# Self-attention's causal mask written into PSUM by TensorE instead of added by VectorE

## The chip, the cores and the metric

The kernel runs on one core of one Trainium2 chip. The metric is the device time of one execution in microseconds; the time given for a kernel is the median of several executions.

## What is computed

Three layers are applied to x (8 sequences of 64 tokens, width 512): a decoder block, a delta-rule attention layer and a mixture of experts. The change touches only the first part of the decoder block, its causal self-attention with 16 heads of width 32:

```
q, k, v = x @ Wq, x @ Wk, x @ Wv + bv          # per head
scores = (q @ k.T) * 32 ** -0.5
scores = where(tril(ones(64, 64)), scores, -inf)
p = softmax(scores)
sa = p @ v
x = layernorm(sa + x, g1, be1)
```

After it come cross-attention to 1601 tokens of context, a feed-forward layer, the delta-rule layer and the experts. All data are float32.

## The kernel before, in words

Every engine runs a list of instructions written out by hand, and semaphores join the lists; nothing is reordered by a planner. Of this kernel only the functions `pe_self`, `dve_self` and `act_self` matter here. They hold the list of TensorE (PE), of VectorE (DVE) and of ScalarE (ACT) for self-attention.

The 512 tokens are taken in four tiles, t = 0 to 3, of 128 tokens: a tile is two sequences, `j` = 0 and 1. The 16 heads are split as 4 blocks of width 128 (`c`) of 4 heads (`i`). The scores of a tile stand in `sc`, which is four PSUM banks: bank `i` holds, in its first 256 columns, the heads `(i, c)` side by side, 64 columns each, and the rows 0 to 63 are the first sequence, 64 to 127 the second. So one tile's scores are 128 rows by 1024 values.

For one tile the steps are:

1. `scores(t)` on PE: 32 small matmuls write the 16 heads of two sequences into `sc` (L368). There is one set of banks, so PE may start the next tile only after VectorE has read this one: it waits for `s1_masked`.
2. `shifted(t)` on DVE, three instructions: scores plus mask, from PSUM into `s1` in SBUF (L258); the negated maximum of each row and head (L261, `nmax`); `s1` plus that maximum (L262), which releases `s1_ready`.
3. `exponentials(t)` on ACT: `p1` = exp of `s1` (L312).
4. `turn_probs(t)` on PE: eight transposes of `p1` into the two ring banks (L384); ACT copies them to `pT1` (L327).
5. `outputs(t)` on PE: small matmuls with the values (L399) into the banks `turnbank` and `pv`.
6. `normalised(t)` on DVE: reciprocal and product (L276, L277), the residual (L282), layernorm statistics (L163, L164), and the affine part (L177, L181), with two small GpSimd (POOL) steps for the root in between (L168, L169). It releases `normed`.

PE's list is: projections of q and k (L358), `scores(0)`, `values(0)`, `values(1)` (the projection of v, L374), `scores(1)`, `values(2)`, `values(3)`, and then for t = 0 to 3 `turn_probs(t)`, `scores(t + 2)` while there is one, `outputs(t)`. Behind it stand two early pieces of cross-attention's key projection (L598) and the transposes of the normed tiles (L423), which wait for `normed`.

DVE's list is: `shifted(0)`, a split of a weight matrix, copies of the values, `shifted(1)`, copies of the values, and then for t = 0 to 3 `shifted(t + 2)` while there is one, `normalised(t)`. ACT's list has, in its loop over t, the copies to `pT1` first and `exponentials(t + 2)` behind them.

The mask is built early by GpSimd in SBUF: 0 where a token may look and -3.0e38 elsewhere, 128 rows by 4 x 64 columns, so it is right for one bank as it stands. `ident` is a 128 by 128 identity in SBUF, used by every transpose.

Of the kernel before, what the change touches and what calls it, by code (L numbers as in the profile page):

```python
# [16 lines left out]
ALU = mybir.AluOpType  # L17
ACT = mybir.ActivationFunctionType
AX = mybir.AxisListType

P = 128
B, S, D = 8, 64, 512
TOK = B * S
NT = TOK // P
NC = D // P
H, E = 16, 32
# [4 lines left out]
G = 256  # L31
# [11 lines left out]
def build(nc, a, out):  # L43
# [4 lines left out]
    def sem(name):  # L48
        if name not in sems:
            sems[name] = ctx.enter_context(nc.semaphore(name))  # L50
        return sems[name]
# [3 lines left out]
    def at(name, offset, shape, dt=F32):  # L55
        return nc.alloc_sbuf_tensor_at(name, shape, dt, offset=base + offset)


    sc = ctx.enter_context(nc.psum_tensor("sc", [P, 4, 512], F32))
# [6 lines left out]
    ident = at("ident", 0, [P, P])  # L66
# [38 lines left out]
    kT1 = at("kT1", R + 8192, [P, NC, TOK])  # L105
# [3 lines left out]
    mask = at("mask", R + 79872, [P, NC, S])  # L109
# [9 lines left out]
    s1 = at("s1", R + 188992, [P, 1024])  # L119
# [27 lines left out]
    def over_tiles(v, n=NT):  # L147

        return v.unsqueeze(1).to_broadcast([v.shape[0], n, v.shape[1]])

    def over_width(v, w):

        return v.unsqueeze(2).to_broadcast([v.shape[0], v.shape[1], w])
# [8 lines left out]
    def norm_stats(dve, link, src, t):  # L162
        link(dve.bn_stats(stat[:, t, :], src[:, t, :]))  # L163
        dve.bn_aggr(mv[:, t, :], stat[:, t, :]).then_inc(sem("variance_ready"), 1)  # L164
# [6 lines left out]
    def norm_apply(dve, n, dst, src, t):  # L171

        dve.wait_ge(sem("rstd_ready"), norm_count(n, t))
        return dve.tensor_scalar(dst[:, t, :], src[:, t, :], mv[:, t, 0:1], rstd[:, t:t + 1], ALU.subtract, ALU.mult)
# [8 lines left out]
    def norm_affine(dve, link, n, dst, src, t, gain, shift):  # L183

        dve.wait_ge(sem("variance_ready"), norm_count(n, t))
        link(norm_center(dve, src, t, gain))
        return norm_shift(dve, n, dst, src, t, shift)
# [32 lines left out]
    def values_copies(eng, copy, t):  # L220

        eng.wait_ge(sem("self_proj_done"), 2 * NC + t + 1)
        for dst, to, of in ((v1, 0, 0), (v1s, 0, S), (v1s, S, 0)):
            n = P if dst is v1 else S
            copy(dst[to:to + n, t, :, 0:E], bank[4 + t][of:of + n, :].rearrange("p (h e) -> p h e", h=H))\
                .then_inc(sem("v1_copied"), 1)

    def dve_self(dve, link):
        dve.wait_ge(sem("x_loaded"), 16)
        for t in range(NT):  # L230
            norm_stats(dve, link, xin, t)
        for t in range(NT):
            norm_apply(dve, 0, xa, xin, t).then_inc(sem("normed"), 1)

        for c in (0, 1):
            dve.wait_ge(sem("turned"), 1)
            dve.tensor_copy(nT[:, c, :], bank[c]).then_inc(sem("turned_copied"), 1)
        dve.wait_ge(sem("rows_loaded"), 64)
        dve.wait_ge(sem("normed"), NT)
        link(dve.tensor_tensor(xa[:, :, :], xa[:, :, :], over_tiles(bv1[:, :]), ALU.add))  # L240
        for c in (0, 1):
            dve.wait_ge(sem("self_proj_done"), c + 1)
            dve.tensor_scalar(qT1[:, c, :], bank[c], SCALE, None, ALU.mult).then_inc(sem("self_qk_copied"), 1)
        dve.wait_ge(sem("split_high"), 1)
        dve.tensor_tensor(wk_l[:, :, :], wk2[:, :, :], wk_h[:, :, :].bitcast(F32), ALU.subtract).then_inc(sem("split_low"), 1)
        for c in (0, 1):
            dve.wait_ge(sem("self_proj_done"), NC + c + 1)
            dve.tensor_copy(kT1[:, c, :], bank[4 + c]).then_inc(sem("self_qk_copied"), 1)

        nmax16 = nmax[:, :, :].rearrange("p a b -> p (a b)")  # L250

        def shifted(t):
            dve.wait_ge(sem("scores_done"), t + 1)
            if t > 0:
                dve.wait_ge(sem("p1_ready"), t)
            else:
                dve.wait_ge(sem("mask_ready"), 2)
            dve.tensor_tensor(s1[:, :].rearrange("p (i k) -> p i k", i=4), sc[:, :, 0:G],  # L258
                              over_tiles(mask[:, :, :].rearrange("p c k -> p (c k)"), 4), ALU.add).then_inc(sem("s1_masked"), 1)
            dve.wait_ge(sem("s1_masked"), t + 1)  # L260
            link(dve.tensor_reduce(nmax16, s1[:, :].rearrange("p (h k) -> p h k", h=H), AX.X, ALU.max, negate=True))  # L261
            dve.tensor_tensor(s1[:, :].rearrange("p (h k) -> p h k", h=H), s1[:, :].rearrange("p (h k) -> p h k", h=H),  # L262
                              over_width(nmax16, S), ALU.add).then_inc(sem("s1_ready"), 1)

        shifted(0)
        dve.wait_ge(sem("split_high"), 2)
        dve.tensor_tensor(wv_l[:, :, :], wv2[:, :, :], wv_h[:, :, :].bitcast(F32), ALU.subtract).then_inc(sem("split_low"), 1)
        values_copies(dve, dve.tensor_copy, 0)
        shifted(1)
        values_copies(dve, dve.tensor_copy, 2)  # L270

        def normalised(t):
            dve.wait_ge(sem("outputs_done"), 2 * (t + 1))
            for q in (0, 1):
                out = bank[6 + q][:, 0:8 * (E + 1)].rearrange("p (m e) -> p m e", e=E + 1)
                link(dve.reciprocal(rinv[:, q, :], out[:, :, E]))  # L276
                dve.tensor_tensor(sa[:, t, :].rearrange("p (m q n) -> p m q n", m=2, q=2)[:, :, q, :].rearrange("p m (i e) -> p m i e", i=4),  # L277
                                  out[:, :, 0:E].rearrange("p (m i) e -> p m i e", m=2),
                                  rinv[:, q, :].rearrange("p (m i) -> p m i", m=2).unsqueeze(3).to_broadcast([P, 2, 4, E]),
                                  ALU.mult).then_inc(sem("sa_written"), 1)  # L280
            dve.wait_ge(sem("sa_written"), 2 * (t + 1))
            link(dve.tensor_tensor(sa[:, t, :], sa[:, t, :], xa[:, t, :], ALU.add))  # L282
            norm_stats(dve, link, sa, t)
            norm_affine(dve, link, 1, xa, sa, t, g1[:, :], be1[:, :]).then_inc(sem("normed"), 1)

        for t in range(NT):
            if t + 2 < NT:
                shifted(t + 2)
            normalised(t)
        dve_jobs(dve, EARLY)  # L290
        for c in (0, 1):
            dve.wait_ge(sem("turned"), 2)
            dve.tensor_copy(nT[:, c, :], bank[c]).then_inc(sem("turned_copied"), 1)
# [51 lines left out]
    def pe_self(pe):  # L345
# [14 lines left out]

        def scores(t):
            if t > 0:
                pe.wait_ge(sem("s1_masked"), t)
            for c in range(NC):
                for j in (0, 1):
                    for i in range(4):
                        rows, b = slice(E * i, E * i + E), 2 * t + j
                        m = pe.matmul(sc[S * j:S * j + S, i, c * S:(c + 1) * S], qT1[rows, c, b * S:(b + 1) * S],  # L368
                                      kT1[rows, c, b * S:(b + 1) * S], start=True, stop=True)
            m.then_inc(sem("scores_done"), 1)  # L370

        def values(t):
# [30 lines left out]

        pe.wait_ge(sem("self_qk_copied"), 2 * NC)
        scores(0)
        pe.wait_ge(sem("matrix2_loaded"), 16)
        values(0)
        values(1)
        scores(1)
        values(2)  # L410
        values(3)
        for t in range(NT):
            turn_probs(t)
            if t + 2 < NT:
                scores(t + 2)
            outputs(t)
# [402 lines left out]
    def dve_jobs(dve, jobs):  # L819

        for k in jobs:
            if k % 2:
                dve.wait_ge(sem("job_done"), k + 1)
                dst, src = job_views(k)
                dve.tensor_copy(dst, src).then_inc(sem("job_copied_v"), 1)  # L825
# [1399 lines left out]
```

## Time and profile before

| | |
|---|---|
| median of 3 runs | 1516.21 us (1515.05 to 1517.49) |
| time of the profiled execution | 1516.03 us |
| its span in the trace | 1514.8 us |
| PE busy | 1455.1 us, 96% |
| DVE busy | 746.1 us, 49% |
| ACT busy | 561.8 us, 37% |
| share of TensorE in the chain that ended last | 88% |

The span runs from the first to the last instruction in the trace, and 1.2 us lie around it. A busy PE is one that has an instruction in it, not one at its peak. The "PEclk" line is TensorE's granted clock in tenths of full speed.

### The profile page before, as it was taken

The numbers are of one execution on the slowest core, as the hardware profiler recorded it, in microseconds if no ns is written. First come the engines' busy times: TensorE is split into PE (matmuls) and PEld (weight loads), VectorE is DVE, ScalarE is ACT, GpSimd is POOL, SyncE is SP. The second block draws the span as 40 slices with busy tenths as digits, with TensorE's granted clock in tenths as the row PEclk, the third lists the DMA queues.
The fourth block names the chain that finished last, engine by engine and source line by source line (L and its number), as shares of the span: only waits on it lengthen the run. The fifth ranks groups of instructions, "written<-read, shape, count | busy, mean of one in ns | idle before, by whom it ended". The sixth has DMA issues, their size and how long they took to land.

```text
span 1514.8 us, 30228 instructions
## 1 busy us (share of the span) xinstructions
PE 1455.1 (96%) x12960; PEld 1066.0 (70%) x12960; DVE 746.1 (49%) x1288; ACT 561.8 (37%) x1179; POOL 253.1 (17%) x290
## 2 busy tenths in 40 slices
PE   9799899999999999999999998998989999999998
PEld 5469788888888888888878776786478744444444
DVE  3632232443544544535346466545976544444444
ACT  1323333344343443434444444451523133333332
POOL 1223222212121212121212230602061000000000
PEclk9889999999999999999999999999999999999999
DMA  7012211010101010101011035305100069999992
GB/s 263 2 35 89 67 46 43 22 46 22 47 22 43 26 43 22 47 22 46 22 43 47 24 129 200 105 0 211 39 3 30 32 219 347 347 347 347 348 346 83
DMA packets 85218, 159.97 MB, mean 106 GB/s; under 512 B 4576, under 2 KB 25056, under 8 KB 85088
## 3 DMA queue, kind: packets, MB, share of 16 engines
q1 hardware_dynamic: 85088, 158.06, 29.9%
q8 instruction: 104, 1.70, 0.5%
q14 instruction: 26, 0.21, 0.0%
HBM read 157.00 MB, written 1.05 MB: 104 GB/s over the span
## 4 chain that ended last, share of the span: by engine, by line
PE 88%; DVE 7%; ACT 2%; POOL 2%; issue 1%; DVEq 0%; ACTq 0%; POOLq 0%
PE ring L598 18%; PE ring L608 18%; PE ring L1972 7%; PE turnbank L644 6%; PE pv L2027 6%; PE pv L1972 4%; PE sc L625 4%; PE pv L663 3%; PE sc L1572 3%; PE sc L1140 3%; PE ring L1152 1%; POOL x_l L562 1%; PE sc L2043 1%; PE sc L358 1%; PE sc L431 1%
## 5 line engine op out<-in xcount | busy, mean ns | idle before, releaser
L562 POOL TENSOR_TENSOR x_l<-raw,x_h 128x384 fp32r<-128x384 f32 (+1 forms) x160 | 162.4, 1047 | 696.6 <-ACT x_h L555 696.4
L598 PE MATMUL ring<-x_h,wk_h 128*128 128x384 f32 (+1 forms) x512 | 186.9, 365 | 5.5 <-POOL x_l L562 5.5
L608 PE MATMUL ring<-wv_h,x_h 128*128 128x512 f32 (+2 forms) x520 | 191.4, 368 | 0.0
L752 ACT ACTIVATE prob<-sc,nm 128x384 f32<-128x384 f32 (+1 forms) x256 | 154.0, 612 | 98.7 <-DVE nm L846 56.5
L608 PE MATMUL ring<-wv_h,x_l 128*128 128x512 f32 (+2 forms) x520 | 181.6, 349 | 0.0
L608 PE MATMUL ring<-wv_l,x_h 128*128 128x512 f32 (+2 forms) x520 | 181.0, 348 | 0.0
L841 DVE TENSOR_REDUCE nm<-sc 128x2 f32<-128x898 f32 (+1 forms) x128 | 128.0, 1021 | 102.4 <-PE sc L625 102.4
L598 PE MATMUL ring<-x_h,wk_l 128*128 128x384 f32 (+1 forms) x512 | 177.2, 346 | 0.0
L598 PE MATMUL ring<-x_l,wk_h 128*128 128x384 f32 (+1 forms) x512 | 176.9, 346 | 0.0
L644 PE MATMUL turnbank<-ident,prob 128*128 128x128 f32 x880 | 137.0, 278 | 12.9 <-DVE pT L832 7.1
L832 DVE COPY pT<-turnbank 128x512 f32<-128x512 f32 x126 | 86.7, 688 | 101.6 <-PE turnbank L644 101.2
L644 PEld LDWEIGHTS turnbank<-ident,prob 128*128 128x128 f32 x880 | 103.1, 141 | 28.3 <-issue 9.2
L598 PEld LDWEIGHTS ring<-x_h,wk_h 128*128 128x128 f32 x512 | 97.6, 191 | 30.9 <-issue 29.2
L608 PEld LDWEIGHTS ring<-wv_h,x_h 128*128 128x128 f32 (+1 forms) x520 | 96.4, 185 | 27.6 <-issue 16.6
L1972 PE MATMUL ring<-w_raw,disp 128*64 128x512 f32 (+1 forms) x640 | 115.0, 596 | 0.0
L608 PEld LDWEIGHTS ring<-wv_h,x_l 128*128 128x128 f32 (+1 forms) x520 | 96.3, 185 | 14.7
L608 PEld LDWEIGHTS ring<-wv_l,x_h 128*128 128x128 f32 (+1 forms) x520 | 96.7, 186 | 11.4 <-issue 0.2
L598 PEld LDWEIGHTS ring<-x_l,wk_h 128*128 128x128 f32 x512 | 97.7, 191 | 1.6
L598 PEld LDWEIGHTS ring<-x_h,wk_l 128*128 128x128 f32 x512 | 97.3, 190 | 1.8
L742 ACT COPY pT<-turnbank 128x512 f32<-128x512 f32 x94 | 55.1, 586 | 96.7 <-PE turnbank L644 96.1
L825 DVE COPY v<-ring 128x512 f32<-128x512 f32 (+3 forms) x65 | 38.0, 584 | 106.1 <-PE ring L608 106.1
L825 DVE COPY kT<-ring 128x384 f32<-128x384 f32 (+1 forms) x64 | 36.7, 574 | 99.5 <-PE ring L598 99.3
(475 smaller groups left out, 2324.6 us busy)
## 6 DMA issues: line engine op xcount, KB each, us to landing
w_raw<-in_ew SPq DMA_DIRECT2D x96, 1024.0 KB, 11.1
raw<-in_ctxT SPq DMA_DIRECT2D x30, 768.0 KB, 4.3
raw<-in_ctxT SPq DMA_DIRECT2D x10, 900.0 KB, 4.7
wf1b<-in_wf SPq DMA_DIRECT2D x1, 2560.0 KB, 10.6
wf2b<-in_wf SPq DMA_DIRECT2D x1, 2560.0 KB, 16.8
wf1a<-in_wf SPq DMA_DIRECT2D x1, 1536.0 KB, 9.4
wf2a<-in_wf SPq DMA_DIRECT2D x1, 1536.0 KB, 12.8
xin<-in_x SPq DMA_DIRECT2D x1, 1024.0 KB, 5.7
```

The lines of the kernel that those rows point to most:

```text
L562: pool.tensor_tensor(x_l[x % 3][:, c, 0:w], raw[x % 3][:, c, 0:w], x_h[x % 2][:, c, 0:w].bitcast(F32), ALU.subtract)\
L598: m = pe.matmul(ring[k % 2][:, 0:w], wt[:, c, e:e + P], xt[:, c, 0:w], start=c == 0 and n == 0, stop=c == NC - 1 and n == 2)
L608: m = pe.matmul(ring[k % 2][0:rows, 0:cols.stop - cols.start], xt[:, c, t1:t1 + rows], wt[:, c, cols], start=c == 0 and n == 0, stop=c == ...
L625: m = pe.matmul(sc[S * j:S * j + S, i, FIRST[r]:FIRST[r] + w], qT[rows, c, b * S:(b + 1) * S], kT[b % 2][rows, c, BASES[r][j]:BASES[r][j] ...
L644: m = pe.transpose(turned_bank(i)[0:w, s * P:(s + 1) * P], prob[:, head, t0:t0 + w], ident[:, :])
L742: act.copy(dst, src).then_inc(sem("turned_a"), 1)
L752: act.activation(prob[:, i, 0:WIDTHS[r]], sc[:, i, score_columns(r)], ACT.Exp, bias=nm[:, b % 2, r, h:h + 1], accum_out=psum[:, b % 2, r, ...
L825: dve.tensor_copy(dst, src).then_inc(sem("job_copied_v"), 1)
L832: dve.tensor_copy(dst, src).then_inc(sem("turned_v"), 1)
L841: ins = dve.tensor_reduce(new, sc[:, 2 * i:2 * i + 2, score_columns(r)], AX.X, ALU.max, negate=True)
L1972: k = pe.matmul(out, disp[:, c, columns], w_raw[n % NSLOT][:, c, :], start=c == 0, stop=c == NC - 1)
L2027: k = pe.matmul(down_bank[0:CAP, :], ht[:, 4 * q + f, :], wt[:, f, :], start=q == 0 and f == 0 and i == 0, stop=q == 3 and f == 3 and i == 2)
```

## The change

Before each tile's scores, TensorE now writes the mask into the four banks: one matmul for each bank, with the identity as the weights and the mask as the moving operand, 128 rows by 256 columns. The 32 small score matmuls then add to what stands in the bank (start is false). VectorE's addition of the mask is gone: the maximum is taken from PSUM, and the difference is formed from PSUM into `s1`. The banks are now free for the next tile only after that last step, so PE waits for `s1_ready` in place of `s1_masked`; the wait for `p1_ready` stands before the difference and not before the first instruction.

```diff
         def shifted(t):
             dve.wait_ge(sem("scores_done"), t + 1)
+            by_head = sc[:, :, 0:G].rearrange("p i (c k) -> p i c k", c=NC)
+            link(dve.tensor_reduce(nmax16, by_head, AX.X, ALU.max, negate=True))
             if t > 0:
                 dve.wait_ge(sem("p1_ready"), t)
-            else:
-                dve.wait_ge(sem("mask_ready"), 2)
-            dve.tensor_tensor(s1[:, :].rearrange("p (i k) -> p i k", i=4), sc[:, :, 0:G],
-                              over_tiles(mask[:, :, :].rearrange("p c k -> p (c k)"), 4), ALU.add).then_inc(sem("s1_masked"), 1)
-            dve.wait_ge(sem("s1_masked"), t + 1)
-            link(dve.tensor_reduce(nmax16, s1[:, :].rearrange("p (h k) -> p h k", h=H), AX.X, ALU.max, negate=True))
-            dve.tensor_tensor(s1[:, :].rearrange("p (h k) -> p h k", h=H), s1[:, :].rearrange("p (h k) -> p h k", h=H),
-                              over_width(nmax16, S), ALU.add).then_inc(sem("s1_ready"), 1)
+            dve.tensor_tensor(s1[:, :].rearrange("p (i c k) -> p i c k", i=4, c=NC), by_head,
+                              over_width(nmax16, S).rearrange("p (i c) k -> p i c k", i=4), ALU.add).then_inc(sem("s1_ready"), 1)
...
         def scores(t):
             if t > 0:
-                pe.wait_ge(sem("s1_masked"), t)
+                pe.wait_ge(sem("s1_ready"), t)
+            else:
+                pe.wait_ge(sem("mask_ready"), 2)
+            for i in range(4):
+                pe.matmul(sc[:, i, 0:G], ident[:, :], mask[:, :, :].rearrange("p c k -> p (c k)"), start=True, stop=False,
+                          skip_group_check=True)
             for c in range(NC):
                 for j in (0, 1):
                     for i in range(4):
                         rows, b = slice(E * i, E * i + E), 2 * t + j
                         m = pe.matmul(sc[S * j:S * j + S, i, c * S:(c + 1) * S], qT1[rows, c, b * S:(b + 1) * S],
-                                      kT1[rows, c, b * S:(b + 1) * S], start=True, stop=True)
+                                      kT1[rows, c, b * S:(b + 1) * S], start=False, stop=True, skip_group_check=True)
```

On TensorE, from the last value projections to the first outputs, the list before is this (one row for each kind of instruction, with what it waits for; `ring<-ident,p_101` are the transposes of `turn_probs(0)`, and L399 is where `outputs(0)` begins):

```order
L374 MATMUL ring<-w_in_98,nT 128x512 x7
L368 MATMUL sc<-kT_91,qT_90 64x64 [waits s1_masked]
L368 MATMUL sc<-kT_91,qT_90 64x64 x31
L374 MATMUL turnbank<-w_in_98,nT 128x512 x4
L374 MATMUL pv<-w_in_98,nT 128x512 x4
L384 MATMUL ring<-ident,p_101 128x128 [waits v1_copied,p1_ready]
L384 MATMUL ring<-ident,p_101 128x128 x7
L368 MATMUL sc<-kT_91,qT_90 64x64 [waits s1_masked]
L368 MATMUL sc<-kT_91,qT_90 64x64 x31
L399 MATMUL turnbank<-v_105,pT_108 64x33 [waits ones_ready,probs_copied]
```

In the changed kernel the same place on TensorE reads so:

```order
L375 MATMUL ring<-w_in_98,nT 128x512 x7
L363 MATMUL sc<-mask,ident 128x256 [waits s1_ready]
L363 MATMUL sc<-mask,ident 128x256 x3
L369 MATMUL sc<-kT_91,qT_90 64x64 x32
L375 MATMUL turnbank<-w_in_98,nT 128x512 x4
L375 MATMUL pv<-w_in_98,nT 128x512 x4
L385 MATMUL ring<-ident,p_101 128x128 [waits v1_copied,p1_ready]
L385 MATMUL ring<-ident,p_101 128x128 x7
L363 MATMUL sc<-mask,ident 128x256 [waits s1_ready]
L363 MATMUL sc<-mask,ident 128x256 x3
L369 MATMUL sc<-kT_91,qT_90 64x64 x32
L400 MATMUL turnbank<-v_105,pT_108 64x33 [waits ones_ready,probs_copied]
```

Four mask matmuls stand before each tile's scores, behind the same instructions as the scores before; nothing else on TensorE has moved.

On VectorE, `shifted(2)` and the beginning and the end of `normalised(0)` stand in the list before as follows:

```order
L258 TENSOR_TENSOR s_107<-sc,mask 128x1024 [waits p1_ready,scores_done]
L261 TENSOR_REDUCE nmax<-s_107 128x16 [waits s1_masked]
L262 TENSOR_TENSOR s_107<-s_107,nmax 128x1024 [waits dve_chain]
L276 RECIPROCAL rinv<-turnbank 128x8 [waits outputs_done]
...
L181 SCALAR_TENSOR_TENSOR xa<-sa,rstd,be_94 128x512 [waits rstd_ready,dve_chain]
L258 TENSOR_TENSOR s_107<-sc,mask 128x1024 [waits p1_ready,scores_done]
```

In the changed kernel the same stretch of VectorE's list is this:

```order
L255 TENSOR_REDUCE nmax<-sc 128x16 [waits scores_done]
L258 TENSOR_TENSOR s_107<-sc,nmax 128x1024 [waits p1_ready,dve_chain]
L272 RECIPROCAL rinv<-turnbank 128x8 [waits outputs_done]
...
L181 SCALAR_TENSOR_TENSOR xa<-sa,rstd,be_94 128x512 [waits rstd_ready,dve_chain]
L255 TENSOR_REDUCE nmax<-sc 128x16 [waits scores_done]
```

One instruction of three is gone from each tile, and the order of the others is as it was.

## Rows read from the trace of the kernel before

**Rows 1.** The page: busy time, the granted clock in 40 slices, the chain's shares.

```profile
PE 1455.1 (96%) x12960; PEld 1066.0 (70%) x12960; DVE 746.1 (49%) x1288; ACT 561.8 (37%) x1179; POOL 253.1 (17%) x290
...
PEclk9889999999999999999999999999999999999999
...
PE 88%; DVE 7%; ACT 2%; POOL 2%; issue 1%; DVEq 0%; ACTq 0%; POOLq 0%
```

**Rows 2.** Busy time by stretch; columns: stretch, length, engines' busy time, clock, DMA.

```profile
0.00:58.00 58.00, 54.37 (x296) 29.84 (x296) 27.01 (x33) 13.54 (x15) 6.22 (x22) 1.00 0.51 172
58.00:92.40 34.40, 23.47 (x459) 21.52 (x459) 24.61 (x44) 9.79 (x16) 12.67 (x16) 0.70 0.02 4
92.40:1514.80 1422.40, 1377.22 (x12208) 1014.69 (x12206) 694.45 (x1212) 538.44 (x1149) 234.18 (x253) 0.99 0.30 105
```

**Rows 3.** The chain that ended last, 40 to 95 us; start, length, what.

```profile
42.28 0.91 PE sc L368 x53
43.19 7.06 PE ring L374 x16
...
54.73 3.45 PE pv L374 x8
...
60.14 1.11 PE ring L384 x8
61.24 1.24 PE sc L368 x60
...
62.50 1.24 DVE s L258
...
65.02 1.50 DVE s L262
66.52 0.13 DVE rinv L276
...
71.63 1.23 DVE s L258
...
75.41 0.94 issue
76.35 1.06 ACT pT L327 x2
...
84.40 6.21 PE ring L598 x24
90.61 1.75 PE sc L423 x16
```

**Rows 4.** Timeline, DVE and POOL, 43 to 91 us; start, length, instruction.

```profile
43.23 1.23 DVE L258 TENSOR_TENSOR s<-sc,mask 128x1024 f32<-128x1024 f32 x1 [7.76 <-PE sc L368]
...
44.48 1.22 DVE L261 TENSOR_REDUCE nmax<-s 128x16 f32<-128x1024 f32 x1
...
45.74 1.23 DVE L262 TENSOR_TENSOR s<-s,nmax 128x1024 f32<-128x1024 f32 x1
...
63.48 1.96 POOL L562 TENSOR_TENSOR x_l<-raw,x_h 128x384 fp32r<-128x384 f32 x2
...
90.16 0.75 DVE L181 SCALAR_TENSOR_TENSOR xa<-sa,rstd,be 128x512 f32<-128x512 f32 x1 [0.82 <-POOL rstd L169]
```

**Rows 5.** Timeline of PE: matmuls that bound the price of the new ones.

```profile
1.58 8.81 PE L343 MATMUL pv<-ident 128*128 128x128 f32 x56 [1.58 <-POOL ident L201]
...
92.31 0.28 PE L608 MATMUL ring<-wv_l,x_h 128*128 128x256 f32 x1
92.43 0.28 PE L608 MATMUL ring<-wv_h,x_l 128*128 128x256 f32 x1
```

**Rows 6.** Busy time and granted clock (third from last) by stretch, as Rows 2.

```profile
60.14:61.03 0.89, 0.89 (x8) 0.82 (x8) 0.00 (x0) 0.89 (x1) 0.89 (x2) 1.00 0.00 0
61.03:67.85 6.82, 6.48 (x202) 5.57 (x200) 5.17 (x8) 2.73 (x5) 4.29 (x5) 0.50 0.02 5
170.26:173.67 3.41, 3.41 (x14) 3.16 (x12) 0.56 (x1) 0.00 (x0) 0.00 (x0) 0.50 0.02 5
173.67:177.09 3.42, 3.42 (x38) 2.38 (x40) 2.16 (x3) 1.46 (x4) 0.00 (x0) 1.00 0.00 0
```

## The prediction, made before the changed kernel ran

> **What bounds the kernel now.** I read the page first: TensorE is busy for 96% of the span and holds 88% of the chain that ended last, VectorE 7% [rows 1]. That average says nothing of self-attention, which lies in the first 92 us. The busy time by stretch shows three stages [rows 2]. Up to 58 us TensorE has 54.4 us of work in 58. From 58.0 to 92.4 us it has 23.5 in 34.4, at a mean clock of 0.70, and VectorE has more than it, 24.6. From 92.4 us to the end TensorE is full again (1377 of 1422 us). So a delay that reaches 92.4 us is handed on whole: behind it one dense list of TensorE runs to the end, and the context loads that it needs start from `normed`, so they move along with it. What the change is worth is what it does to the time of the last transposes (L423).
>
> The chain of work in this piece gives the path [rows 3]. From 42.28 to 58.18 us it is TensorE alone: `scores(0)` 0.91 us, values 7.06, `scores(1)` and the rest of the values, the last of them 54.73 + 3.45. ScalarE's copies of the last values lead to `turn_probs(0)` at 60.14 and `scores(2)` at 61.24. At 62.50 the path goes over to VectorE: `shifted(2)` (62.50 to 66.52), `normalised(0)` (66.52 to 71.63), `shifted(3)` (71.63 to 75.37). Then the chain goes by ScalarE and TensorE, whose copies to `pT1` are queued behind `exponentials(3)`; but VectorE works on beside it without a gap that matters, and its last `normed` comes at 90.16 + 0.75 = 90.91 [rows 4], when TensorE's early projections (84.40 + 6.21 = 90.61) are just done. Both ways begin at the end of `shifted(3)`, so they shift as one.
>
> **The change part by part.** The path to 92.4 us has four pieces that change.
>
> *Mask matmuls of tiles 0 and 1.* They stand in the stretch where TensorE alone is the path, behind a wait that ends where it ended before, and nothing covers them. What does a matmul of 256 float32 columns with the full array cost? The trace shows no such instruction. It shows a float32 matmul as two records; with 512 columns eight records take 3.45 us, 0.431 each [rows 3]. From below: the 256-column matmuls of L608, on numbers rounded for the fast pass, follow each other at 92.43 - 92.31 = 0.12 us with one record each, so four masks would cost 0.48 us [rows 5]. From above: the keep-busy matmuls, float32 with the identity as weights and 128 columns, take 8.81 / 56 = 0.157 us a record, more than a quarter of 0.431; if 128 more columns add another 0.108, a record is 0.265 and four masks cost 8 x 0.265 = 2.12 us. The nearest row is the plain float32 matmul of the same engine on the same kind of data, and half its columns are 0.215 us, which is above the 0.157 that loading the identity seems to need. I take 0.215: eight records are 1.72 us for a tile, 3.44 us for two. VectorE's saving in these tiles is on no path: `s1_ready` of tile 1 is not waited for until 60.14.
>
> *Mask matmuls of tile 2.* They stand between `turn_probs(0)` and `scores(2)`, on the path again. At full clock they are 1.72 us. But the granted clock is 1.00 (2.4 GHz) from 60.14 to 61.03 and 0.50 (1.2 GHz) from 61.03 to 67.85, after TensorE stood idle from 58.2 to 60.1 and during the transposes [rows 6]. The idle piece and the transposes are the same in the changed kernel, 3.44 us later, so the fall comes about at the end of the transposes and the masks run at half clock. Dense full-array matmuls got the clock back sooner than the small ones here: from 170.26 it was at half for 3.41 us and then full [rows 6]. So of the eight records at 0.43 us, 3.2 us go at half clock and the last half record at full; that is 3.3 us. `scores(2)` then takes 0.91 as in tile 0 and not 1.24: 0.33 back [rows 3]. The value is 3.3 - 0.33 = 3.0 us. Bounds: 1.72 - 0.33 = 1.4 if the clock stays full, and 3.43 if half clock outlasts it all.
>
> The Trainium skill's page "TensorE: Matmul & The Clock Gate" (section on PE-mode transpose) says that transposes don't count as activity for the clock gate. The trace agrees in that the clock fell 0.9 us into the transposes. By that rule the masks, which are no transposes, would be the first work that counts after the idle piece; it changes no term.
>
> *Mask matmuls of tile 3.* These I cost at nothing. `scores(3)` now waits for the end of `shifted(2)`, then needs 1.72 + 0.91 us, or 3.43 + 1.28 = 4.7 at half clock. What hides it is `normalised(0)` on VectorE, 71.63 - 66.52 = 5.11 us, which stands ahead of `shifted(3)`. Queued behind the wait is `outputs(1)`; it ends some 75 us into the span at the latest, and VectorE asks for it only after `shifted(3)`, at about 79. Without that cover the cost would be the whole 1.7 to 3.4 us.
>
> *VectorE's savings.* Two of the four `shifted` are on the path, tiles 2 and 3. Each loses one instruction of three: 63.76 - 62.50 and 72.88 - 71.63, 1.25 us from start to start, 2.5 us for the two. Is the rest slower from PSUM? The three forms take 1.23 (from PSUM), 1.22 and 1.23 us (both from SBUF) [rows 4], so I add nothing. L262 of tile 2 took 1.50 us beside a split on GpSimd that ran until 65.44 [rows 4]; by my times that split ends before, so 0.27 us more is saved: 2.8 us in all. From below the saving is 2.5.
>
> The Trainium skill's page "VectorE: DVE Perf Modes" (section on the errata) gives VectorE a fixed cost of 120 cycles with a source in PSUM and of 58 from SBUF. The mask addition from PSUM against the difference from SBUF shows 0.00 us in this trace, not 0.065. By the page the four instructions from PSUM would add 4 x 0.065, less the one that was there in each tile: an estimate of 0.13 us more.
>
> *Sum.* 3.44 + 3.0 - 2.8 = +3.6 us. Against the profiled execution's own 1516.03 us that gives 1519.6; the median of the runs is 0.2 us above that execution, which I leave aside.
>
> **The rivals.**
>
> *The clock stays up at tile 2 (not slower).* Whether the clock falls before, in or behind the masks hangs on a moment that can lie otherwise than in the one execution that I see: the three runs are 2.4 us apart. With the masks and `scores(2)` at full clock the sum is 3.44 + 1.4 - 2.8 = +2.0 us, 1518.0. It decides below +3.03 us (0.2% of 1516, about what can be told from no change): that is when less than about half of the masks fall on half clock. For it: the masks are dense, and begin 1.1 us after the idle piece ends. Against it: the clock fell exactly there before.
>
> *The masks cost more than half of a 512-column matmul.* At 0.265 us a record, as bounded above, tiles 0 and 1 cost 4.24 us and tile 2 some 0.4 more: 3.6 + 0.8 + 0.4 = +4.8, 1520.8. Against it: the identity's own load seems to need no more than 0.157 us.
>
> *The masks are nearly free.* At 0.12 us for a whole matmul, tiles 0 and 1 cost 0.96 us and tile 2 about 0.5 to 1.0, and the VectorE savings win: 0.96 + 0.7 - 2.8 = -1.1, 1514.9. Against it: every plain float32 matmul in the trace shows two records at four times the pace of the rounded ones. Even with masks at nothing the gain is no more than 2.8 to 3.1 us, so "faster by over 0.2%" needs them free and something more.
>
> *The moved wait becomes the bound.* If the masks of tile 3 run at half clock and at the higher price (4.2 + 1.28 = 5.5 us against 5.11), `shifted(3)` starts 0.4 us late: 3.6 + 1.2 + 0.4 = +5.2, 1521.2.
>
> **How the numbers follow.** The first forecast has 0.52, with +3.2 to +4.1 as its own range (3.4 for tile 2 at most, and the small doubt on the 0.27); an execution where the clock falls midway lies between it and the full-clock rival, which has 0.28. The higher price has 0.09, the nearly free masks 0.06, the late wait 0.05. The range is 1517.4 to 1521.4: it takes in the first two, the higher price, and a microsecond either way for the spread of the runs. What a measurement of this kernel can tell from no change is about 0.2%, 3.03 us. Slower by more: most of the first (0.40 of 0.52, since 3.6 lies near the limit), the higher price and the late wait, with 0.01 of the second: 0.53. Faster by more: 0.03, from the nearly free masks and what I don't see. Within 0.2%: 0.44.
>
> **What would show it.** In the changed kernel's trace: (1) the four masks of tiles 0 and 1 are eight records each, 0.215 us from start to start, and `turn_probs(0)` starts at about 63.6 us; (2) the masks of tile 2 begin at about 64.7 us with the granted clock at 0.50, `scores(2)` ends at about 68.9; (3) `shifted` is two instructions of 1.22 to 1.23 us; (4) `shifted(3)` starts straight behind `normalised(0)`, not behind a wait for TensorE; (5) the last transposes start about 3.6 us later than 90.61. The prediction is wrong if the clock behaves otherwise in (2), if reading PSUM twice costs VectorE more, or if the stage behind 92.4 us takes up the delay, for which I see no room.

## The result, and the profile after

| | before | changed |
|---|---|---|
| median, 12 runs each | 1515.93 us (1515.05 to 1517.49) | 1518.74 us (1517.76 to 1521.63) |
| profiled execution | 1516.03 us | 1518.77 us |
| its span | 1514.8 us | 1517.5 us |

The ratio is 1.002 with a 95% interval of 1.0012 to 1.0028: the change costs 2.8 us, and between 1.8 and 4.2 us by the interval. Against the limit of 0.2% it is neither clearly within nor clearly beyond it.

The chain of work of the changed kernel, from 40 to 98 us (start, length, what), answers to [rows 3]:

```profile
42.48 1.99 PE sc L363 x8
...
45.32 7.06 PE ring L375 x16
52.38 1.73 PE sc L363 x8
...
65.06 1.73 PE sc L363 x8
...
67.67 1.24 DVE nmax L255
...
68.93 1.22 DVE s L258
...
75.26 1.23 DVE nmax L255
...
76.51 1.24 DVE s L258
...
86.78 6.24 PE ring L599 x24
93.02 1.75 PE sc L424 x16
94.77 1.43 PE ring L609 x12
```

Three groups of mask matmuls (L363) are on it, and VectorE's part is two steps for each tile. The last transposes start at 93.02 instead of 90.61, 2.41 us later. Its steps in order: 0.20 us later already at 42.48, before anything is changed (the 13 traces of this document reach this place between 42.11 and 42.54); the stretch from there to the values (45.32) is 2.84 us and was 0.91, so tile 0 costs 1.93; tile 1 costs 1.73 in the same way; from `turn_probs(0)` (64.00) to VectorE's start (67.67) it is 3.67 us and was 2.36, so tile 2 costs 1.31; `shifted(2)` is 1.54 us shorter (67.67 to 70.15, before 62.50 to 66.52) and `shifted(3)` 1.25. The sum is 0.20 + 1.93 + 1.73 + 1.31 - 1.54 - 1.25 = +2.38 us, and 0.03 more at the transposes. The span is 2.7 us longer. Most of the other 0.3 us appears at one place: at 1195.8 us VectorE sits idle for 0.27 us between two of its own instructions, and for 0.03 us at the same place before. Why is open.

The groups of instructions of self-attention after the change (line, engine, operation, tiles, count, busy time, mean ns of one, idle before) show the new prices beside [rows 4] and [rows 5]:

```profile
L363 PE MATMUL sc<-mask,ident 128*128 128x256 f32 x32 | 7.8, 386 | 1.2 <-ACT kT L302 0.7 <-DVE s L258 0.5
...
L258 DVE TENSOR_TENSOR s<-sc,nmax 128x1024 f32<-128x1024 f32 x4 | 4.9, 1224 | 0.1
L255 DVE TENSOR_REDUCE nmax<-sc 128x16 f32<-128x1024 f32 x4 | 4.9, 1222 | 19.5 <-PE sc L369 19.5
```

The reduction and the difference from PSUM take 1.22 us each, as they did from SBUF. The granted clock is the third number from the end in the busy time by stretch; these two rows answer to [rows 6]:

```profile
64.00:77.12 13.12, 10.68 (x296) 8.96 (x296) 8.35 (x13) 4.34 (x6) 5.21 (x6) 1.00 0.01 2
77.12:90.77 13.65, 9.77 (x149) 9.24 (x150) 11.41 (x26) 3.09 (x5) 2.68 (x4) 0.50 0.01 3
```

In this execution the clock did not fall at tile 2. It stayed at 2.4 GHz through the masks, and fell to 1.2 GHz at 77.12, while TensorE stood idle (75.2 to 79.8). It waited there for ScalarE's copies, which are queued behind `exponentials(3)` and so behind `shifted(3)`.

### The profile page after: what moved, and what is told of

It reads as the page before. It is cut to its first block, busy times and chain, and to the rows that moved or that the text cites. A ratio compares the mean times of both kernels' runs of the same rounds, so it can differ in the third digit from the quotient of the medians.

```text
span 1517.5 us, 30288 instructions
## 1 busy us (share of the span) xinstructions
PE 1460.7 (96%) x12992; PEld 1070.2 (71%) x12992; DVE 741.3 (49%) x1284; ACT 561.8 (37%) x1179; POOL 252.2 (17%) x290
## 4 chain that ended last, share of the span: by engine, by line
PE 88%; DVE 7%; ACT 2%; POOL 2%; issue 1%; DMA 0%; DVEq 0%; ACTq 0%
PE ring L599 18%; PE ring L609 18%; PE ring L1973 7%; PE turnbank L645 6%; PE pv L2028 6%; PE pv L1973 4%; PE sc L626 4%; PE pv L664 3%; PE sc L1573 3%; PE sc L1141 3%; PE ring L1153 1%; POOL x_l L563 1%; PE sc L2044 1%; PE sc L354 1%; PE sc L432 1%
```

## The experiments

Where a run's difference is called that of the median, it is against the kernel before in the same series (1516.47 us for the first four, 1515.99 for the next four); where it is called that of the trace, it is the start of the transposes of the normed tiles against 90.61.

### TensorE's part alone

The mask matmuls are added to the kernel before, and VectorE keeps its addition.

```diff
-MASKED = -3.0e38
+MASKED = -1.0e38
...
             if t > 0:
                 pe.wait_ge(sem("s1_masked"), t)
+            else:
+                pe.wait_ge(sem("mask_ready"), 2)
+            for i in range(4):
+                pe.matmul(sc[:, i, 0:G], ident[:, :], mask[:, :, :].rearrange("p c k -> p (c k)"), start=True, stop=False,
+                          skip_group_check=True)
...
-                                      kT1[rows, c, b * S:(b + 1) * S], start=True, stop=True)
+                                      kT1[rows, c, b * S:(b + 1) * S], start=False, stop=True, skip_group_check=True)
```

> The mask matmuls are added and VectorE keeps its own addition too, so the mask is added twice (its fill is -1.0e38 here, so that the sum stays finite; the output is the same). My theory: TensorE's part alone costs 3.7 us at tiles 0 and 1 and 1.3 us (full clock) to 3.0 us (half clock) at tile 2, so +5.0 to +6.7 us against the kernel before. The rival that the cost lies in VectorE's reads of PSUM expects no more than +3 us here. A granted clock of 0.50 on the masks of tile 2 in this profile, against 1.00 in the changed kernel's, would speak for the moment of the fall lying differently from execution to execution.

Measured: 1521.63 us, +5.2 by the median, ratio 1.0032 (1.0023 to 1.0041). In its chain of work the last transposes start at 95.51, +4.9:

```profile
65.11 1.73 PE sc L367 x8
...
67.72 1.24 DVE s L258
...
70.24 1.23 DVE s L262
...
95.51 1.75 PE sc L428 x16
```

The last `normed` is +4.95: 0.26 of a later start at 42.54 (42.28 before), 1.93 + 1.73 + 1.31 from TensorE, less 0.27 from L262, which takes 1.23 us here and 1.50 before: GpSimd's split, which ran beside its first 0.42 us before, ends here at 69.36, before it starts. The cost of the change is TensorE's.

### VectorE's part alone

`shifted` as changed, and TensorE as before; no mask is applied.

```diff
         def shifted(t):
             dve.wait_ge(sem("scores_done"), t + 1)
+            by_head = sc[:, :, 0:G].rearrange("p i (c k) -> p i c k", c=NC)
+            link(dve.tensor_reduce(nmax16, by_head, AX.X, ALU.max, negate=True))
...
         def scores(t):
             if t > 0:
-                pe.wait_ge(sem("s1_masked"), t)
+                pe.wait_ge(sem("s1_ready"), t)
```

> VectorE's part alone: two instructions from PSUM, and no mask matmuls on TensorE, so the mask is left out of the computation. My theory: tiles 2 and 3 save 1.25 us each, and 0.27 us where the difference no longer stands beside GpSimd's split: -2.5 to -2.8 us. The rival that reading PSUM twice costs VectorE more than SBUF (0.13 us in all by the Trainium skill) expects -2.4 us; a rival in which VectorE is not the path in this stage expects 0.

Measured: 1511.85 us, -4.6 by the median, ratio 0.9966 (0.9953 to 0.9979). This is more than expected. The median rests on five runs; the profiled execution is 4.2 us faster than the profiled one of before, 3.96 of it at the start of the last transposes. The chain of work and the clock by stretch say where these are from:

```profile
61.91 1.24 DVE nmax L255
...
69.50 1.23 DVE nmax L255
...
81.01 5.64 PE ring L594 x24
86.65 1.75 PE sc L419 x16
```

```profile
59.97:73.52 13.55, 7.08 (x280) 6.14 (x280) 10.39 (x18) 5.85 (x9) 5.24 (x6) 1.00 0.01 2
73.52:83.76 10.24, 8.51 (x145) 7.99 (x146) 8.16 (x19) 1.59 (x4) 2.69 (x4) 0.50 0.01 4
```

VectorE starts tile 2 at 61.91, 0.59 us earlier: 0.17 us is a start that was earlier all along, and 0.4 us is the clock, which here stayed at 1.00 through `scores(2)`, although TensorE's instructions from the idle piece to `scores(2)` are those of the kernel before. From there VectorE gains 2.8 us by the end of `shifted(3)`, as expected. The last 0.6 us are TensorE's early projections, 5.64 us instead of 6.21, because the clock came back at 83.76, 2.75 us after they began, and in the kernel before 3.9 us after. This speaks for a fall at tile 2 that belongs to an execution and not to the kernel; the last three runs test that on one kernel.

### The change at two tiles at a time

`BY_PE` names the tiles that TensorE masks; the others are masked by VectorE as before, but TensorE waits for `s1_ready` at all of them. The diff is a part of that of the first kernel; the second has (2, 3).

```diff
+BY_PE = (0, 1)
+HOISTED = ()
...
+        def masks(t):
+            if t > 0:
+                pe.wait_ge(sem("s1_ready"), t)
+            else:
+                pe.wait_ge(sem("mask_ready"), 2)
+            for i in range(4):
+                pe.matmul(sc[:, i, 0:G], ident[:, :], mask[:, :, :].rearrange("p c k -> p (c k)"), start=True, stop=False,
+                          skip_group_check=True)
+
         def scores(t):
-            if t > 0:
-                pe.wait_ge(sem("s1_masked"), t)
+            own = t not in BY_PE
+            if own:
+                if t > 0:
+                    pe.wait_ge(sem("s1_ready"), t)
+            elif t not in HOISTED:
+                masks(t)
...
-                                      kT1[rows, c, b * S:(b + 1) * S], start=True, stop=True)
+                                      kT1[rows, c, b * S:(b + 1) * S], start=own, stop=True, skip_group_check=True)
```

> The change at tiles 0 and 1 only, tiles 2 and 3 as before. My theory: TensorE's masks there stand on the path and VectorE's saving is hidden, so +3.7 us, and nothing in the traces differs behind 64 us but the shift. Rival: part of it is taken up by the idle piece of TensorE ahead of the first transposes: then under +2 us.

Measured: 1519.95 us, +3.5 by the median, ratio 1.0024 (1.0016 to 1.0033); by the trace +3.88. The whole loss of the change, and more, is at tiles 0 and 1. Its clock fell 0.9 us after `turn_probs(0)` began at 64.02, as in the kernel before:

```profile
64.02:64.91 0.89, 0.89 (x8) 0.83 (x8) 0.00 (x0) 0.89 (x1) 0.00 (x0) 1.00 0.00 0
64.91:71.74 6.83, 6.55 (x202) 5.58 (x200) 5.19 (x8) 2.73 (x5) 3.87 (x4) 0.50 0.01 2
```

> The change at tiles 2 and 3 only, tiles 0 and 1 as before. My theory: VectorE saves 2.8 us, the masks of tile 2 cost 1.3 us at full clock or 3.0 at half: -1.5 us or +0.2 us. The rival that the whole change is a loss in each tile expects +1 us or more. If the clock falls during the masks here, as it fell in the kernel before at the same place, the execution profiled shows about +0.2 us; if it stays up, dense matmuls keep it up.

Measured: 1515.70 us, -0.8 by the median, ratio 0.9991 (0.9982 to 1.0); by the trace -1.72 where -1.5 was expected for full clock. The clock stayed up at tile 2, VectorE's `shifted(3)` ends 1.3 us earlier, and 0.4 us is again the early projections' clock (5.77 us instead of 6.21). At tiles 2 and 3 the change is no loss by these runs; whether it is a gain the median can't tell.

### The masks twice

```diff
-            for i in range(4):
+            for i in [0, 1, 2, 3] * 2:
                 pe.matmul(sc[:, i, 0:G], ident[:, :], mask[:, :, :].rearrange("p c k -> p (c k)"), start=True, stop=False,
```

> The changed kernel with each tile's four mask matmuls issued twice; the second four overwrite the first, so the output is the same. My theory: another 3.5 us at tiles 0 and 1 (16 records at 0.215), 1.7 us at tile 2 at full clock or up to 3.4 at half, and at tile 3 nothing or little, since 3.45 + 0.9 = 4.4 us stands beside 5.1 us of VectorE: 5.2 to 6.9 us more than the changed kernel, +8 to +10 us against the kernel before. If the clock had stayed up by the masks' density, it stays up here. A rival with a fixed cost for the switch from full to tiled matmuls expects less, about +3.5 us more.

Measured: 1522.07 us, +6.1 by the median, ratio 1.0047 (1.0033 to 1.0061). The chain of work:

```profile
42.34 3.72 PE sc L363 x16
...
46.90 7.06 PE ring L375 x16
53.96 3.45 PE sc L363 x16
...
68.37 3.46 PE sc L363 x16
...
72.70 1.23 DVE nmax L255
...
80.29 1.23 DVE nmax L255
```

The second four cost 1.72 to 1.73 us in each of tiles 0, 1 and 2, so the price is 0.216 us a record and not a fixed cost of switching. Tile 3's sixteen records cost nothing: `normalised(0)` is the cover, and `shifted(3)` starts 7.59 us after `shifted(2)`, 2.48 and 5.11, as in the changed kernel. The last `normed` comes 7.4 us later than before and 5.0 later than in the changed kernel, where 5.2 to 6.9 was expected. The total has less of it and misses the expected +8 to +10: it is 3.3 us over the changed kernel by the two medians' distances from the kernel before, and taken alone that would fit the rival of a fixed cost. The trace decides against this rival, since each of three tiles pays for its second four in full. Of what is missing, 0.7 us is at the early projections; in the profiled execution, which is 4.6 us slower than that of before, another 2.0 is behind 98 us, where it lacks the pieces at half clock that the kernel before has from 170, 884 and 955 us. The five runs are 4 us apart.

### The masks of tile 2 moved into the idle piece

`masks` holds the wait and the four mask matmuls; `scores(2)` no longer issues them.

```diff
+BY_PE = (0, 1, 2, 3)
+HOISTED = (2,)
...
+        masks(2)
         for t in range(NT):
             turn_probs(t)
             if t + 2 < NT:
                 scores(t + 2)
```

> The changed kernel with the masks of tile 2 moved ahead of the first transposes, into the 2 us in which TensorE waits for ScalarE's copies. My theory: 1.7 us (or more, where the clock fell) come back, and the clock falls later or not at all: about +1.0 us against the kernel before, -1.7 to -2 us against the changed one. Rival: tile 2's masks are hidden anyway or come back as another wait: no difference from the changed kernel.

Measured: 1516.71 us, +0.7 by the median, ratio 1.0005 (0.9996 to 1.0014); by the trace +0.92, and 2.1 us better than the changed kernel, by the two medians' distances from the kernel before. By the trace it is 1.5 us better than the changed kernel: the masks end at 63.65, and the transposes start at 63.90 as soon as ScalarE's copies are done; 0.35 us is lost again at the early projections (6.59 us instead of 6.24). The move takes the masks of tile 2 off the path. The clock stayed at 1.00 at tile 2 here and in the last of these versions, where the masks fill the idle piece too; most traces with the piece left idle show the same, so two traces don't tell whether filling it helps.

### Mask and identity in bfloat16

```diff
-                pe.matmul(sc[:, i, 0:G], ident[:, :], mask[:, :, :].rearrange("p c k -> p (c k)"), start=True, stop=False,
+                pe.matmul(sc[:, i, 0:G], ident16[:, :], mask16[:, :, :].rearrange("p c k -> p (c k)"), start=True, stop=False,
```

> The changed kernel with mask and identity in bfloat16 (two more copies on GpSimd, early). The masked values are exp of about -3e38 either way. My theory: a mask matmul is one record at about 0.11 us, so four cost 0.45 us in place of 1.72: tiles 0 and 1 cost 0.9, tile 2 about 0.45 less 0.35 for the faster scores or less: about -1.8 us against the kernel before. Rival: a fixed cost for each mask matmul or each switch: then no better than 0.

Measured: 1514.26 us, -1.7 by the median as expected, ratio 0.9991 (0.9982 to 1.0); by the trace -1.78. Four masks are four records and 0.44 us in the chain of work, against eight and 1.73:

```profile
50.73 0.44 PE sc L367 x4
...
62.11 0.44 PE sc L367 x4
```

### The change where it is on VectorE's path, with TensorE's part under cover

Tiles 2 and 3 are masked by TensorE, the masks of tile 2 ahead of the first transposes; tiles 0 and 1 are as before.

```diff
+BY_PE = (2, 3)
+HOISTED = (2,)
...
+        masks(2)
         for t in range(NT):
             turn_probs(t)
```

> The change at tiles 2 and 3 only, with the masks of tile 2 ahead of the first transposes; tiles 0 and 1 as before, where VectorE's addition is hidden. My theory: VectorE's 2.5 to 2.8 us are saved and TensorE's masks are all under cover: -2.5 to -3.1 us against the kernel before. Rival: the masks in the idle piece delay the transposes or the scores, or the clock costs more: -1.5 us or less.

Measured: 1513.93 us, -2.1 by the median, ratio 0.9985 (0.9976 to 0.9994). By the trace it is -3.63 (the transposes start at 86.98): 2.8 us from VectorE as expected, and 0.8 beyond it, 0.1 of an earlier start, 0.4 of full clock at `scores(2)` and 0.3 at the early projections. This version beats the kernel before by 0.06 to 0.24%; the median falls short of the expected -2.5 to -3.1. In the profiled execution the lead is lost again behind 850 us, and its trace shows where. Taken at the same instructions of VectorE, the lead is 3.71 us up to 883.66, 2.28 from 886.74, 2.49 at 1088.26, 0.79 from 1090.59, and at 1126.18 it is gone. TensorE's clock in these stretches (busy time by stretch) is this:

```profile
879.70:886.52 6.82, 6.51 (x32) 4.75 (x32) 2.58 (x4) 1.82 (x5) 0.00 (x0) 0.50 1.03 398
1084.50:1087.91 3.41, 3.41 (x5) 1.42 (x5) 3.34 (x6) 1.12 (x2) 0.00 (x0) 0.50 0.00 0
1118.63:1125.46 6.83, 6.83 (x93) 6.81 (x95) 5.78 (x6) 1.65 (x5) 6.83 (x5) 0.50 0.01 2
```

The kernel before has at the same places in the program 3.41 us at half clock instead of 6.82, and none at the other two:

```profile
883.64:887.05 3.41, 3.33 (x22) 1.85 (x23) 1.08 (x2) 0.59 (x1) 0.00 (x0) 0.50 1.04 410
1086.98:1090.39 3.41, 3.41 (x9) 1.57 (x9) 3.34 (x6) 1.13 (x2) 0.00 (x0) 1.00 0.00 0
1119.42:1126.25 6.83, 5.05 (x132) 4.93 (x133) 6.19 (x7) 1.73 (x5) 6.83 (x5) 1.00 0.01 2
```

The same can be read in the kernel with VectorE's part alone. Its timeline of VectorE has these two copies, from the same places in the program:

```profile
179.20 0.42 DVE L821 COPY v<-ring 128x256 f32<-128x256 f32 x1 [2.89 <-PE ring L604]
...
188.13 0.62 DVE L821 COPY kT<-ring 128x449 f32<-128x449 f32 x1 [7.80 <-PE ring L594]
```

In the kernel before they are these:

```profile
183.23 0.42 DVE L825 COPY v<-ring 128x256 f32<-128x256 f32 x1 [2.89 <-PE ring L608]
...
190.60 0.62 DVE L825 COPY kT<-ring 128x449 f32<-128x449 f32 x1 [6.24 <-PE ring L598]
```

The lead is 4.03 us and then 2.47. Between them lies a piece at half clock in the one and none in the other; the busy time of the one by stretch and then of the kernel before:

```profile
182.74:186.16 3.42, 3.42 (x11) 3.03 (x10) 0.00 (x0) 0.54 (x1) 0.00 (x0) 0.50 0.06 20
```

```profile
186.00:190.20 4.20, 4.20 (x23) 3.89 (x22) 0.00 (x0) 0.54 (x1) 0.00 (x0) 1.00 0.22 80
```

So one such fall, after a wait of 1.8 us for GpSimd that both kernels have, costs 1.56 us in one execution and nothing in another.

### The changed kernel again, for the clock at tile 2

Three more executions of the changed kernel, with no edit.

> The changed kernel unchanged, one look for its trace. The question is the granted clock at tile 2's masks. Theory A, the moment at which the clock may fall lies differently in each execution: in some of three such looks it is 0.50 on the masks of tile 2, these take up to 3.4 us instead of 1.7, and VectorE's third shifted tile ends about 1.5 us later than in the first trace of this kernel. Theory B, the masks' density keeps it up: it is 1.00 there in all three, and the last transposes start within 0.3 us of 93.0.

> The same kernel and the same question, second look: 0.50 on the masks of tile 2 in some looks (theory A), 1.00 in all (theory B).

> The same kernel and the same question, third look: 0.50 on the masks of tile 2 in some looks (theory A), 1.00 in all (theory B).

Measured: 1520.19, 1519.27 and 1518.50 us; the kernel before ran once beside them, in 1514.83. The second and the third have the clock at 1.00 on the masks of tile 2. In the first it fell 0.99 us after `turn_probs(0)` began. Its clock by stretch and its chain of work:

```profile
63.88:64.87 0.99, 0.99 (x9) 0.99 (x10) 0.00 (x0) 0.99 (x1) 0.00 (x0) 1.00 0.00 0
64.87:68.28 3.41, 3.41 (x17) 2.23 (x15) 0.00 (x0) 1.33 (x3) 2.97 (x4) 0.50 0.00 0
```

```profile
64.94 3.36 PE sc L363 x8
...
69.19 1.24 DVE nmax L255
...
94.46 1.75 PE sc L424 x16
```

The masks take 3.36 us, `scores(2)` is back at full clock, and from `turn_probs(0)` to VectorE's start it is 69.19 - 63.88 = 5.31 us, 2.95 more than before. Theory A holds, and theory B, full clock in all three, falls. The first mask record starts at 64.78 and the clock fell at 64.87, so this trace doesn't say whether masks that had run for longer would have kept the clock up.

## Why the prediction was right, and where it was off

*The path.* Right. Tiles 0 and 1 go onto the total whole (+3.88 by the trace of that kernel alone), VectorE's savings count at tiles 2 and 3 alone, and the delay at the last transposes, 2.41 us, is most of the 2.7 us at the end. "Handed on whole" holds for a pair of executions only up to the clock's falls behind 92.4 us, which moved the other traces by up to 3.6 us.

*Masks of tiles 0 and 1.* Forecast 3.44 us, measured 1.93 + 1.73 = 3.66. The price of a record was right (0.216 us against 0.215). The bound from above was misread: the 0.157 us of the keep-busy matmuls is a mean over two paces. Up to 6.2 us of the trace they start every 0.213 us and from 6.4 us on every 0.111, about half of a 256-column record; the clock column has no entry before 6.41 and so reads 1.00 at both. So no load of the identity of 0.157 us stands behind these numbers, and the record of 0.265 had no ground. Tile 0's 0.2 us more stand in its first record, which follows a wait: 1.99 us for the eight, against 1.73 where they follow other work. The rivals of a higher price and of nearly free masks fall; in bfloat16 the latter's price comes true, 0.44 us for four.

*Masks of tile 2.* This is the step that failed for the typical execution: "the fall comes about at the end of the transposes and the masks run at half clock". In the profiled execution they ran at full clock and cost 1.31 us, not 3.0, which is the first rival. In four traces of the changed kernel the forecast case came once, and there it was right in each part: half clock for 3.41 us, masks 3.36, the whole piece +2.95. The error was to take the fall in the one trace of before as a property of the kernel. The runs' own spread said otherwise: the rival used it, but with a chance of 0.28 that looks too small beside three traces of four. Eleven traces have the same idle piece of 2.0 us and the same transposes behind it. The clock fell 0.9 to 1.0 us into the transposes in three of them: the one of the kernel before, the one of the kernel masked by TensorE at tiles 0 and 1 alone, and the first of the three repeats; of those with masks behind the transposes it is one in eight, of those without two in three. These are too few to say that masks play no part in how often it falls, and what decides it in an execution stays open. What the prediction read as the trace's agreement with a rule on transposes is one trace's: in eight of the eleven the clock stayed up through the same transposes.

*Masks of tile 3.* Right: under `normalised(0)`, 5.11 us before and after, even when doubled.

*VectorE.* Forecast 2.8 us, measured 1.54 + 1.25 = 2.79. Reading both from PSUM costs nothing: 1.222 and 1.224 us against 1.22 and 1.23 from SBUF [rows 4]. The larger fixed cost for PSUM that the Trainium skill's page "VectorE: DVE Perf Modes" gives (section on the errata) is not seen here. The 0.27 us of L262 were saved too, but not as forecast ("by my times that split ends before"): in the changed kernel GpSimd's split still runs until 69.29, beside the start of the difference.

```profile
65.42 3.87 POOL L563 TENSOR_TENSOR x_l<-raw,x_h 128x384 fp32r<-128x384 f32 x4 [1.50 <-ACT x_h L556]
...
68.93 1.22 DVE L258 TENSOR_TENSOR s<-sc,nmax 128x1024 f32<-128x1024 f32 x1
```

With its operand in PSUM the difference takes 1.22 us beside the split, also where it lies wholly beside it (63.17 to 64.39 in the kernel with VectorE's part alone, whose split ends at 65.29). With its operand in SBUF it takes 1.50 and 1.51 us in the two traces where the split ends 0.42 us into it, and 1.23 without. So here the right number came partly by luck.

*The sum.* Forecast +3.6, measured +2.8 by the medians and +2.7 by the profiled executions. Without the half clock at tile 2 the forecast's own terms give +2.0; the first record's 0.2, the start's 0.2 and 0.3 behind 1100 us are the rest. The range held the time, and the chances of 0.44 and 0.53 for within and beyond 0.2% fit a value that lies at that limit (the parts named for "slower by more" add up to 0.55 and not 0.53). The execution with half clock at tile 2 delays the last transposes by 3.85 us, against the forecast 3.6.

## What to carry to other kernels

Work moved from one engine to another should be priced tile by tile: here half of VectorE's savings were hidden, while TensorE's additions were on the path in three tiles of four, and the same edit made only at the tiles where VectorE is the path, with its matmuls put where TensorE waits, gains 2.1 us instead of losing 2.8. A mask put in through PSUM costs a matmul for each bank, and in float32 with 256 columns that is 0.43 us; in bfloat16 it is 0.11. A clock level seen in one trace near a short idle piece should be taken as one draw: look at a second trace of the same kernel, or at the spread of the runs, before a term rests on it. The same goes for a mean over many equal instructions: look whether they keep one pace before it is used as a price.

## What the runs showed of the hardware

- A fall of TensorE's granted clock behind 2 us of idleness and 0.9 us of transposes comes in some executions of the same program and not in others (1 of 4 of the changed kernel). 3.4 us more at half clock cost 1.56, 1.43 and 1.70 us at three places, and 6.8 us more cost 1.13 at a fourth, where TensorE has work for 5.05 of 6.83 us in the kernel before. The runs of one kernel spread by more than one such piece (1515.05 to 1517.49 us before, 1517.76 to 1521.63 after); that the falls make up this spread is likely, and was not counted out.
- Full-array masks that begin at 64.8 us, just before the fall, ran 3.4 us at 1.2 GHz and the clock then rose; where the work after the fall was transposes and small tiled matmuls it stayed down for 6.8 us [rows 6].
- Adding to a PSUM bank by the 32-row score matmuls costs what overwriting it does: `scores(t)` is 0.84 us in both kernels at full clock.
- VectorE's difference with its operand in SBUF took 1.50 us where GpSimd's split ran beside its start, and 1.22 us with its operand in PSUM; a reduction from SBUF that lay wholly beside the split took 1.22 us (L261 at 63.76). That the split is what slowed it is argued from these rows, and no run took the split away.
